# The planner's look-ahead window W in an eight-core attention-plus-FFN kernel, from 250 to 800 operations

## The reference

```python
def _phi(x): return jax.nn.elu(x) + 1.0
# attention, on xn = layernorm(x); q, k, v per head by 64x64 weights
qf, kf = _phi(q), _phi(k)
kv = einsum('bhsd,bhse->bhde', kf, v);  z = sum(kf, axis=2)      # over the whole sequence
ctx = einsum('bhsd,bhde->bhse', qf, kv) / (einsum('bhsd,bhd->bhs', qf, z) + 1e-6)
attn = ctx @ Wo
x = x + layernorm(attn)
# feed-forward, on h = layernorm(x); three 1024x1024 weights in a row
x = x + layernorm(tanh(h @ weight @ aux_weight1 @ aux_weight2 + bias))
```

## Time and profile before

| | us |
|---|---|
| median of 2 runs | 1031.71 |
| lowest, highest | 1031.57, 1031.84 |
| the profiled execution, device time | 1034.02 |
| its span, slowest core (core 6) | 1032.5 |
| spans of its cores | 1025.4 to 1032.5 |
| granted TensorE clock, cores | 0.754 to 0.766 |

### The profile page before, as it was taken

One profiled execution on the slowest core, in us unless ns is written; L12 is line 12 of the kernel. 1 busy time (PEld: TensorE's weight loads), 2 busy tenths in 40 slices (PEclk: granted clock), 3 DMA queues, 4 the chain that ended last, 5 costly groups with the idle time before them and its releaser, 6 DMA issues.

```text
span 1032.5 us, 10998 instructions; the slowest of 8 cores (1025.4 to 1032.5 us)
## 1 busy us (share of the span) xinstructions
PE 595.7 (58%) x3352; PEld 309.1 (30%) x3392; DVE 538.5 (52%) x914; ACT 453.0 (44%) x769; POOL 222.7 (22%) x154
## 2 busy tenths in 40 slices
PE   0503467774575765765684546455757657755752
PEld 0402343232332332332332334332323323322321
DVE  1313523224655765566766454346657755665553
ACT  1824971002333453343444799733433533434233
POOL 3445000001032322221311200011323222223132
PEclk9755779997776876877678666767668768777787
DMA  6867310000111111111112332001111110111010
GB/s 192 282 238 271 104 40 1 1 0 1 41 62 41 56 47 61 41 42 62 61 52 92 118 109 81 21 1 41 57 45 42 61 62 30 53 61 42 1 41 41
DMA packets 20764, 69.53 MB, mean 67 GB/s; under 512 B 2129, under 2 KB 4305, under 8 KB 20706
## 3 DMA queue, kind: packets, MB, share of 16 engines
q1 hardware_dynamic: 11490, 35.27, 10.6%
q0 software_dynamic: 6912, 25.17, 6.6%
q10 hardware_dynamic: 2304, 8.39, 2.2%
HBM read 52.04 MB, written 16.78 MB: 67 GB/s over the span
## 4 chain that ended last, share of the span: by engine, by line
PE 29%; DVE 22%; ACT 22%; issue 13%; DMA 7%; POOL 6%; DVEq 1%; ACTq 0%; SPq 0%; POOLq 0%
PE PS_C L724 10%; PE PS_B L764 6%; DMA stage<-a 5%; DVE big_b L740 4%; DVE ln_bn L475 4%; POOL big_b L700 4%; DVE ln_bn L473 3%; PE PS_C L616 3%; PE PS_C L630 3%; ACT big_b L501 2%; DVE big_b L696 2%; ACT big_b L776 2%; DVE big_b L496 2%; ACT big_b L778 2%; PE PS_A L675 2%
## 5 line engine op out<-in xcount | busy, mean ns | idle before, releaser
L700 POOL TENSOR_TENSOR big_b<-big_b 128x1024 bf16<-128x1024 bf16 x32 | 74.4, 2325 | 447.4 <-DVE big_b L696 410.9
L484 ACT ACTIVATE ln_l<-ln_ag,eps_s 128x1 f32<-128x1 f32 x128 | 38.2, 299 | 300.4 <-DVE ln_ag L477 286.4
L764 PE MATMUL PS_B<-p_b,big_b 128*128 128x512 bf16 x500 | 147.3, 461 | 31.9 <-DVE big_b L753 29.9
L724 PE MATMUL PS_C<-wo_b,big_b 128*128 128x512 bf16 x490 | 152.7, 479 | 10.2 <-issue 6.1
L785 POOL TENSOR_TENSOR out_b<-big_b 128x1024 f32<-128x1024 f32 x32 | 79.9, 2496 | 296.0 <-DVE big_b L496 285.1
L708 PE MATMUL PS_A<-big_b,kvblk_b 128*128 128x128 bf16 x256 | 33.3, 273 | 107.5 <-POOL big_b L700 91.4
L764 PEld LDWEIGHTS PS_B<-p_b,big_b 128*128 128x128 bf16 x512 | 56.4, 115 | 126.2 <-issue 93.9
L724 PEld LDWEIGHTS PS_C<-wo_b,big_b 128*128 128x128 bf16 x512 | 58.3, 119 | 95.4 <-issue 66.9
L563 DVE SCALAR_TENSOR_TENSOR kf_b<-relu_b,exp_b 128x1024 bf16<-128x1024 bf16 x32 | 39.6, 1238 | 90.6 <-ACT exp_b L556 79.2
L740 DVE TENSOR_TENSOR big_b<-x_tm,big_b 128x1024 f32<-128x1024 f32 x32 | 61.0, 1905 | 34.3 <-ACT big_b L501 31.0
L523 PE MATMUL PS_T<-eye_b,xn_tm 128*128 128x128 bf16 x256 | 27.9, 275 | 84.2 <-ACT xn_tm L501 44.1
(11 more groups left out here) (70 smaller groups left out, 1086.1 us busy)
## 6 DMA issues: line engine op xcount, KB each, us to landing
x_tm<-x SPq DMA_DIRECT2D x64, 512.0 KB, 3.7
y<-out_b POOLq DMA_DIRECT2D x32, 512.0 KB, 3.0
stage<-a POOLq DMA_DIRECT2D x16, 512.0 KB, 6.2
stage<-wt ACTq DMA_DIRECT2D x8, 512.0 KB, 6.9
stage<-wo ACTq DMA_DIRECT2D x8, 512.0 KB, 5.4
stage<-wkvblk SPq DMA_DIRECT2D x2, 512.0 KB, 7.4
stage<-wqblk SPq DMA_DIRECT2D x1, 512.0 KB, 8.6
stage<-eye SPq DMA_DIRECT2D x1, 64.0 KB, 1.8
```

The costliest lines, as they stand in the source:

```text
L700: p.op("gpsimd", lambda e: e.tensor_tensor(qf2_b[j], qf_b[j], rdenbc_b[j], ALU.mult), reads=[("qf", j), ("rdenbc", j, 0), ("rdenbc", j, 1) ...
L724: p.op("tensor", lambda e, cc=c, h2=hh: e.matmul(PS_C[:, h2 * 512:(h2 + 1) * 512], ctx_b[j][:, cc * 128:(cc + 1) * 128], wo_b[:, cc * 1024 ...
L764: p.op("tensor", lambda e, cc=c, h2=hh: e.matmul(PS_B[:, h2 * 512:(h2 + 1) * 512], xn2f_b[j][:, cc * 128:(cc + 1) * 128], p_b[:, cc * 1024 ...
```

## The change

The default of W, the number of operations past the frontier that the planner looks at, goes from 250 to 800. No operation is added, removed or altered; what can differ is the order in which each engine runs its own operations, and which waits they need for it.

```diff
         import os
-        W = int(os.environ.get("KSCHED_W", "250"))
+        W = int(os.environ.get("KSCHED_W", "800"))
         LO = int(os.environ.get("KSCHED_LO", "0"))
         HI = int(os.environ.get("KSCHED_HI", str(n)))
```

## The result

| | before | after |
|---|---|---|
| median us | 1034.12 (8 runs, 1031.57 to 1040.45) | 994.90 (9 runs, 993.14 to 1009.43) |
| ratio | | 0.9613, 95% interval 0.9591 to 0.9635 |
| profiled execution, span of slowest core | 1032.5 (core 6) | 993.5 (core 7) |
| spans of its cores | 1025.4 to 1032.5 | 985.7 to 993.5 |

The kernel became 3.9% faster, 39 us, where 1004 us (from 1034.0 for the profiled execution) had been forecast with a range of 995 to 1020. A second set of runs of the changed kernel, beside other runs of the kernel before, gave 0.9596 (0.9571 to 0.9621). One of the nine runs, 1009.43 us, was a slow one, with a lower granted clock on four of the cores, and the ratio leaves it out.

A forecast was written before the change was run, and what follows sets the result against it. No engine was full over the span; ScalarE stood behind weight-load issues waiting for GpSimd's casts. 1034.0 - 29.0 + 1.0 = 1006.0 us profiled, median 2.3 us lower: 1004 us, range 995 to 1020.

The forecast's parts named there:

- The cause: Pass 1 at the start: window 250 ends at slot 5, so DMA issues awaiting casts stop ScalarE, 33.9 us of waits.
- the start: Load stretch up to fold: fold's first matmul moves from 150.6 to about 121.6 us, 29.0 us earlier.
- the density of ScalarE's work: Pass 1 beside the weight loads: 88.9 us of ScalarE work packed at 0.894 takes 99.4 us, to 121.3 us.
- my own upper bound: Start: at density 0.953 pass 1 would end at 115.2 us, a gain of 35.1 us.
- The loads: Weight loads in pass 1: hidden behind tile work at no further cost, ending at about 140 us, no new wait.
- Rival A: Weight loads block ScalarE again: 6 rounds at 3 us each give back 18 us, 1022 us; chance 0.15.
- Pass 1 of sequence 1: Scaling side gets further ahead, leaving tiles with k/v work alone at 0.81: 1 us lost, 0 to 2.
- 15 places: Passes 2: `p2_A1` comes earlier by a place, its matmuls needed two tiles later: 0 us.
- 5 us either way for knock-on changes of order: Rest of the span: uncertainty put on the 0 us counted for an earlier `p2_A1`.
- D: Whole kernel gains more, 35 + 3 us, from the start and pass 1 of sequence 1: 996 us or below; chance 0.05.
- the tighter packing: Pass 1 at the start: ScalarE's work packed at 0.953, worth the 35 us part of the larger gain.
- the kinder order in pass 1 of sequence 1: Pass 1 of sequence 1: a better order, worth the 3 us part of the larger gain.

The follow-up runs named there:

- e1: Window 800 only while the weight loads at the start are being placed, 250 after, against the kernel before: ratio 0.9619.
- e5: Window 500 instead of 250 everywhere, against the kernel before: ratio 0.9769.
- e3: Window 800 only with the frontier in pass 1 of sequence 1, 250 elsewhere, against the kernel before: ratio 0.9934.
- three delayed: 3, 6 or 12 extra `kvblk` copies before the last pass 2; old window: 1.0023, 0.9984, 1.0020; window 800: 0.9624, 0.9609, 0.9666, all against the kernel before.
- after_again: The changed kernel, window 800, run once more against the kernel before: ratio 0.9596, median 994.5 us.
- e2: Window 800 only with the frontier in the two passes 2, without the last slots of the first, against the kernel before: ratio 0.9884.
- e4: Window 800, but q's matmul groups (`p2_A1`) taken from no more than 250 past the frontier, against the kernel before: ratio 0.9628.
- e6: Window 250 with the planner's GpSimd cast and load costs corrected to the trace, against the kernel before: ratio 0.9876.
- e7: Window 800 with the planner's GpSimd cast and load costs corrected, against the kernel before: ratio 0.9556, run again 0.9585.
- d12_w800: The changed kernel with twelve more `kvblk` copies on VectorE between pass 1 and pass 2 of sequence 1, against the kernel before: ratio 0.9666.

## Why the prediction was wrong, point by point

**The cause was right.** The window ended at slot 5, pass 1 stood still behind DMA issues on ScalarE's queue, and with W = 800 it does not. e1 has the whole of the 34 us from the window at the loads alone, e5 puts the stop where its reach ends.

**How the miss divides.** The sum had a gain of 28.0 us, 29.0 less 1.0; the mean core got 39.7. Of the 11.7 us between them 5.1 are the start (34.1 for 29.0), 5.0 pass 2a and the last pass (1.8 and 3.2, for which the sum had 0), and 2.0 the junction (1.0 gained for 1.0 lost); fold took back 0.4. The time itself is only 9 us off, since the median before, 1031.71 us from two runs, became 1034.12 with eight.

**The term that was mis-sized: the density of ScalarE's work.** I took 0.894 for all of pass 1, from the first 32 us of ScalarE's work, and called it the price of running beside the loads. This is the step that failed. The windows after show that it isn't that price: beside the loads, at 202 GB/s, ScalarE is busy 34.72/36 = 0.964. The 0.894 belongs to the first tiles: up to 56 us the kernel before has 4.1 us of ScalarE's waits for matmuls (line 539) and statistics (lines 477, 491), the changed kernel from 56 to 92 us has 0.8. With 28.8 us done by 54 us, as in both kernels, and the other 60.1 us at the 0.953 of the earlier trace rows, pass 1 ends at 54 + 63 = 117 us, where it did (117.7 on core 7; fold's first matmul at 117.3 there, before that evacuation had quite ended). Over all of ScalarE's pass 1 the density came to 0.92. The step was worth 4 us on the slowest core and 5 on the mean one; my forecast for fold was 121.6, my own upper bound for the gain 35.1. Put simply, the gain at the start, 34.1 us on the mean core, is the 33.9 us of waits, and I had talked myself below it. With the upper bound the same sum gives 998 us, inside the range.

**The loads: right.** No waits for casts, last cast of `wo` starting at 132.3 us (about 140 forecast), of `a2` at 116.2 (needed at 165 by my account, at 160.8 in fact), fold's length 83.0 us on the slowest core (82.2 before, 82 forecast). Rival A got nothing. The pairs of loads stand further apart than the 2.9 tiles that I had worked out: on ScalarE's queue of core 7 the last two loads of `wt` are issued at 71.9 and 80.8 us, the first of `wo` at 107.2.

**Pass 1 of sequence 1: wrong sign.** I charged it with 1 us lost. In e3, where nothing else differs up to its end, the junction is 2.0 us shorter (85.2 for 87.2). In the changed kernel it is 1.0 us shorter, but this can't be booked to the order: e1, with the old order there, has 86.3 us against the changed kernel's 86.2. So the new order gave 2.0 us behind the late start of fold and 0.1 behind the early one, and lost nothing in either. The argument, more k/v work alone at the end, at 0.81, priced a tail and left out that the work ahead of it is taken off something; what makes the 2.0 us in e3 was not looked into.

**Pass 2: the effect was seen and counted as nothing.** I found 15 places where the window held `p2_A1` back "for a few choices only". But one choice made otherwise changes those after it: 300 places of pass 2 of sequence 0 and 271 of the last one differ between the two kernels. Pass 2a shows what that is worth: 350.2 to 350.5 us in five kernels with the old order (before, e3, three delayed) and 352.1 in e1, 347.3 to 348.6 in seven with the new one (after, after_again, e2, e5, three delayed). The ranges don't meet. But the kernels of each group are not independent tests: the old order met two starts of fold in this pass (114.5 and about 149 us), the new one three (115, 134 and 149 us), and no delay was put ahead of it. At an equal start the order is worth 3.5 us (e1 352.1, the changed kernel 348.6) and 3.1 us (350.4 before, e2 347.3); the pair measured here got 1.8, since with either order the pass is 1 to 2 us longer behind the early start.

The groups of GpSimd's two large operations over the whole span, first of the kernel before, then of the changed one, show part of how:

```profile
L700 POOL TENSOR_TENSOR big_b<-big_b 128x1024 bf16<-128x1024 bf16 x32 | 74.4, 2325 | 447.4 <-DVE big_b L696 410.9
...
L785 POOL TENSOR_TENSOR out_b<-big_b 128x1024 f32<-128x1024 f32 x32 | 79.9, 2496 | 296.0 <-DVE big_b L496 285.1
...
L700 POOL TENSOR_TENSOR big_b<-big_b 128x1024 bf16<-128x1024 bf16 x32 | 67.7, 2116 | 424.0 <-DVE big_b L696 319.7
...
L785 POOL TENSOR_TENSOR out_b<-big_b 128x1024 f32<-128x1024 f32 x32 | 76.5, 2390 | 250.1 <-DVE big_b L496 250.1
```

The same operations take 2116 and 2390 ns in the mean, after 2325 and 2496: they meet VectorE's less often. Of the 32 products of line 700, 7 take 3.09 us in core 6 of the kernel before, each with a two-input instruction of VectorE in its first 1.1 us; in core 7 of the changed kernel none takes more than 2.13. One of the seven, core 6 of the kernel before:

```profile
320.13 1.38 DVE L740 TENSOR_TENSOR big_b<-x_tm,big_b 128x1024 f32<-128x1024 f32 x1 [1.54 <-ACT big_b L501]
...
320.40 3.09 POOL L700 TENSOR_TENSOR big_b<-big_b 128x1024 bf16<-128x1024 bf16 x1
```

It was not tried whether this or q's earlier products makes the gain in pass 2a.

**The last pass: open in its share.** The means of the two orders are 357.6 us for seven kernels with the old order (before, e1, e3, e4, three delayed), 355.9 for six with the new (after, e2, e5, three delayed), from 355.0 to 361.3 and from 352.0 to 358.1. (e6, 358.4 us with the old order, and e7, 357.7 and 357.6 with the new one, lie inside them.) The ranges overlap over 3 us, and with six or seven values that spread over 6 us a difference of 1.7 us is not clear of chance. So 1 to 2 us may be the order's, or nothing, and the rest is where this pair happened to fall: luck. I had written "5 us either way for knock-on changes of order"; behind fold pass 2a and the last pass gave 5.0 us in sum, but the point and the range had 0 in them.

**The chances.** 994.9 us is D's time, to which I gave 0.05. Of its two parts the tighter packing came; the kinder order in pass 1 of sequence 1 gave 0.1 us at this start, and pass 2a and the last pass, which D did not have, made up the rest. D's sum was wrong by itself, too: 35 + 3 us off 1034.0 is 996, but the 2.3 us from the profiled execution to the median, which my point had, were left out; with them it is 994 us. The range ended at 995.0 because D was cut off as unlikely, while its main part, density 0.953, stood in my own bounds as a measured value. That the time fell 0.1 us outside the range and not inside is chance: the last pass alone took 355.0 to 361.3 us with one order.

## What to carry to other kernels

When an engine's compute stands still behind a DMA issue in its own queue, read the waits of that stretch as the first estimate of what a reorder gives back; correct it downwards only by a density measured beside the same load in steady state, not in the first tiles. In a list scheduler a look-ahead window binds where one old operation stays unplaced: compute frontier + W in operation numbers there, and expect every later stage to get another order too. And before a gain of 3 us in 1000 is given to an order, shift the stage by a microsecond or two and see whether its length holds.

## What the runs showed of the hardware that I had not expected

**One program, two lengths.** In d12_w800 the last pass takes 355.0 or 358.3 us, core by core, and in the kernel before core 7 needs 357.6 us where the others need 361.7 to 362.0. In e6_costs_w250 six cores take 357.6 or 357.7 us and two 360.9 and 361.0. Within one of these lengths the cores agree to 0.3 us or so. Over seven kernels with nearly the same order it went from 355.0 to 361.3 us, by delays that were not in proportion. Where two cores parted, the granted clock differed over the same matmuls, 0.93 and 0.78.

**Who comes first decides who waits.** In the kernel before, core 0, GpSimd's subtraction and VectorE's phi(q) start within 10 ns, and GpSimd's, the one that starts first by the profile, is stretched; in e1_start_only, core 0, at the same place of the same order, GpSimd is 0.3 us ahead and VectorE's waits it out (timeline; e1's lines are numbered one higher):

```profile
943.12 3.42 POOL L785 TENSOR_TENSOR out_b<-big_b 128x1024 f32<-128x1024 f32 x1 [7.57 <-DVE big_b L496]
...
943.13 1.22 DVE L665 SCALAR_TENSOR_TENSOR big_b<-relu_b,exp_b 128x1024 bf16<-128x1024 bf16 x1
...
908.75 2.33 POOL L786 TENSOR_TENSOR out_b<-big_b 128x1024 f32<-128x1024 f32 x1 [7.26 <-DVE big_b L497]
...
909.05 3.11 DVE L666 SCALAR_TENSOR_TENSOR big_b<-relu_b,exp_b 128x1024 bf16<-128x1024 bf16 x1
```

3.42 us for 2.33, or 3.11 us for 1.22. In the first pair GpSimd's end lies 2.2 us behind VectorE's, about one such instruction alone (2.33); in the second VectorE's end lies 1.1 us behind GpSimd's, again about one (1.22). The Trainium skill (SBUF — State Buffer, SBUF: two separate sides) has it that whichever starts first keeps the shared port for its whole instruction and the other fully blocks. By this rule, the second pair agrees; in the first the one blocked is the one that starts 10 ns ahead, so starts as near as that don't tell who had the port. How that race and the clock share the spread of the last pass is open.
